# Four graph layers on one core: where TensorE transposes rows between rounds one and two, and when ScalarE copies them

## The reference, cut to what matters

```python
deg = segment_sum(ones, dst); dinv = rsqrt(deg); norm = dinv[src] * dinv[dst]
h = relu(segment_sum((x @ W1)[src] * norm[:, None], dst) + b1)
h = relu(segment_sum((h @ W2)[src] * norm[:, None], dst) + b2)
x = layernorm(x + h)
```

## Time and profile before

| | us |
|---|---|
| median of three runs | 4895.24 (4890.82 to 4900.14) |
| the profiled execution | 4889.19 |
| its span | 4887.5 |
| TensorE busy, matmuls | 3164.7 (65%) |
| GpSimd busy | 2620.9 (54%) |
| VectorE busy | 1604.3 (33%) |
| ScalarE busy | 1175.7 (24%) |
| mean granted TensorE clock | 0.748 of full speed |

### The profile page before, as it was taken

One profiled execution on the slowest core, in us unless ns is written; L12 is line 12 of the kernel. 1 busy time (PEld: TensorE's weight loads), 2 busy tenths in 40 slices (PEclk: granted clock), 3 DMA queues, 4 the chain that ended last, 5 costly groups with the idle time before them and its releaser, 6 DMA issues. The chain is left out here.

```text
span 4887.5 us, 63682 instructions
## 1 busy us (share of the span) xinstructions
PE 3164.7 (65%) x23462; PEld 2890.1 (59%) x23462; DVE 1604.3 (33%) x4664; ACT 1175.7 (24%) x1927; POOL 2620.9 (54%) x2640
## 2 busy tenths in 40 slices
PE   1599866885987788443333433355777777777777
PEld 1487755784886678443333323344766677767776
DVE  5588831232223222322212212244222222222224
ACT  4355420001000000122222222233222222222224
POOL 2555425555565555367666666624555555555550
PEclk8699977996998899666565566666777777777776
DMA  3344434664565456311111111112111111111111
GB/s 116 121 165 166 155 140 150 215 224 139 185 224 192 160 187 212 98 33 35 33 36 33 34 35 34 34 30 60 35 34 33 34 34 35 34 33 34 34 34 27
DMA packets 177090, 445.94 MB, mean 91 GB/s; under 512 B 68901, under 2 KB 115386, under 8 KB 156946
## 3 DMA queue, kind: packets, MB, share of 16 engines
q1 hardware_dynamic: 93332, 293.68, 16.6%
q0 software_dynamic: 83456, 148.23, 13.4%
HBM read 350.21 MB, written 91.50 MB: 90 GB/s over the span
## 5 line engine op out<-in xcount | busy, mean ns | idle before, releaser
L1216 PE MATMUL ps<-arena 128*125 128x288 bf16 x7448 | 1181.7, 303 | 171.9 <-issue 122.1
L736 POOL DMA_INDIRECT work_all<-parts_dram,idx_all x832 | 852.9, 1025 | 685.7 <-PE ps L1141 400.7
L1703 POOL DMA_INDIRECT arena<-table,idx_all x832 | 790.6, 950 | 779.7 <-DVE arena L1812 429.0
L1216 PEld LDWEIGHTS ps<-arena 128*125 128x125 bf16 x7448 | 1000.7, 146 | 247.8 <-issue 165.3
L1302 POOL DMA_INDIRECT arena<-table,idx_all x832 | 827.1, 994 | 409.5 <-issue 247.3
L1451 PE MATMUL ps<-arena 128*96 128x128 f32 x1664 | 339.5, 368 | 196.1 <-issue 139.4
L553 DVE TENSOR_TENSOR aggX<-aggX,ps 96x128 f32 x208 | 59.0, 284 | 1189.8 <-remote 730.3
L1451 PEld LDWEIGHTS ps<-arena 128*96 128x96 f32 x1664 | 296.6, 236 | 215.3 <-issue 191.2
L1873 PE MATMUL ps<-M,arena 96*128 96x96 f32 x1664 | 385.1, 329 | 21.5 <-issue 18.6
L1092 PE MATMUL ps<-arena,spare 128*128 128x245 bf16 x950 | 289.9, 312 | 86.6 <-issue 36.2
L1806 DVE COPY arena<-ps 128x1024 bf16<-128x1024 bf16 x104 | 71.9, 692 | 811.6 <-PE ps L1859 466.1
(11 more groups left out here) (341 smaller groups left out, 4860.1 us busy)
## 6 DMA issues: line engine op xcount, KB each, us to landing
arena<-blocks_dram SPq DMA_DIRECT2D x114, 1568.0 KB
blocks_dram<-arena SPq DMA_DIRECT2D x38, 1568.0 KB
arena<-table,idx_all POOLq DMA_INDIRECT x1664
parts_dram<-arena SPq DMA_DIRECT2D x28, 504.0 KB, 3.1
work_all<-parts_dram,idx_all POOLq DMA_INDIRECT x832
arena<-qtable SPq DMA_DIRECT2D x104, 72.0 KB
ea_dram<-arena SPq DMA_DIRECT2D x1, 4992.0 KB, 13.2
arena<-ea_dram SPq DMA_DIRECT2D x1, 4992.0 KB
```

The costliest lines, as they stand in the source:

```text
L736: eng.indirect_dma_start(out=gat_rows[kk % 3][:, u, :], out_offset=None, in_=parts_dram[:, :], in_offset=bass.IndirectOffsetOnAxis(ap=idx_ ...
L1216: last = nc.tensor.matmul(apply_ps[n % 2][0:w, :], blk[m % 3][:, b, 0:w], Hs[:, b, :], start=b == 0, stop=b == NB - 1)
L1703: eng.indirect_dma_start(out=rows[g % NROW][:, u, :], out_offset=None, in_=table[:, :], in_offset=bass.IndirectOffsetOnAxis(ap=idx_all[:, ...
```

## The change

TensorE: `turn` of chunk c-1 is issued behind the product of chunk c, at the end of round one; only that of the last chunk is left at the first block of round two. ScalarE: behind hi(c) and mid(c-1) it copies the transposed rows of chunk c-1, not of chunk c; the last copy is behind mid(6).

```diff
@@ block.scalar, round one
                         for c in range(NCH):
                             hi(r * NCH + c)
                             if c:
                                 mid(r * NCH + c - 1)
-                            turn(r * NCH + c)
+                                turn(r * NCH + c - 1)
                         mid(r * NCH + NCH - 1)
+                        turn(r * NCH + NCH - 1)
                         continue
@@ block.tensor, first block of a round
                                 if p == 0 and b % CB == 0:
                                     c = b // CB
-                                    if r == 2:
-                                        turn(NCH + c)
+                                    if r == 2 and c == 0:
+                                        turn(2 * NCH - 1)
                                     eng.wait_ge(parts_up, (r - 1) * NCH + c + 1)
@@ block.tensor, end of a round
                     eng.wait_ge(acc, n + 1)
                     for c in range(NEARLY if r > 1 else 0, NCH):
                         product(r, c)
+                        if r == 1 and c:
+                            turn(NCH + c - 1)
```

## The result

| | before | after |
|---|---|---|
| median of six runs, us | 4893.98 (4883.07 to 4900.14) | 4856.16 (4851.22 to 4861.00) |
| the profiled execution, us | 4889.19 | 4860.95 |
| its span, us | 4887.5 | 4859.2 |
| last `low` ends, behind the stage's first product | 63.29 | 25.54 |
| first gather of round two starts, behind it | 66.70 | 30.25 |

The ratio is 0.9924, with a 95% interval of 0.9910 to 0.9939. The medians are 37.8 us apart; 4857 was forecast.

A forecast was written before the change was run, and what follows sets the result against it. A ring of waits among TensorE, ScalarE and GpSimd between rounds one and two was the bound. 660.3 + 19.9 + 0.6 + 1.0 = 681.8, + 3.4 + 0.2 = 685.4 against 723.45; 4895.2 - 38 = 4857, upper end 4873, lower 2 us off 4850.

The forecast's parts named there:

- The ring: Between rounds one and two, TensorE, ScalarE and GpSimd wait on each other in turn, 8.04 us a turn.
- GpSimd's sum: Between rounds one and two: fourteen operations 19.9 us, hand-overs 0.6, one-hot 1.0; from 660.3, last low ends at 681.8 us.
- VectorE's one-hot: VectorE's `gathot`, moved to about 675.3 beside GpSimd's work, slows a rem there; 1.0 us taken once.
- TAB writes: VectorE's seven writes beside GpSimd's work between rounds one and two; nothing taken for them.
- The stores: Stores of parts before round two's first gather: 3.4 us plus 0.2 for the last one, gather at 685.4.
- the bound of 3.9 us on landing: A store of parts lands at most 3.9 us after its issue, over all 28; median 3.1.
- TensorE's hold: TensorE's transposes wait for ScalarE's copy three times, about 1.1 us each; products end about 6 us later, costing nothing.
- Rival A: TensorE falls to half clock in the interleaved stretch; last low near 694, gain 26 us, 4869; chance 0.10.
- The rule that transposes don't engage the full rate: For TensorE's interleaved stretch: transposes don't count as activity like matmuls, so it might run slow; no separate size.
- Rival B: GpSimd slowed between rounds one and two, or last stores queueing (3.9 us landing); gain 31 to 32 us, 4864; chance 0.12.
- Rival D: TensorE's instruction stock runs short during round two's gathers; 60 more starved matmuls cost 51 us, 4908; chance 0.03.
- The whole: Whole kernel: first gather of round two from 723.45 to 685.4, gain 38 us, median 4857.

The follow-up runs named there:

- kernel with two areas: The changed kernel with a second PSUM area for the odd chunks' transposes in round two; 4892.80 us, ratio 0.9908 to the kernel before.
- TensorE's extra work: The changed kernel with 49 more transposes on TensorE ahead of round two's first block; 3922.41 us, ratio 0.9906 to the kernel before.
- gaps in the gathers: The changed kernel with GpSimd's gather groups 1 and 2 waiting for TensorE each round; 3942.99 us, ratio 0.9957; on another chip 4831.17 us, 0.9894.

## Why the prediction was right

**The ring.** It was cut as said: GpSimd's pitch went from 8.04 to 3.03 us. The prediction gave both halves of the change a part in it. The runs show that TensorE's half suffices for the stage.

**GpSimd's sum.** Forecast: 21.5 us from first `rem` to last `low`; measured: 682.81 + 2.87 - 663.78 = 21.9. The 1.0 us taken for VectorE's one-hot was 2.44 - 1.46 = 0.98, at a `low` instead of a `rem`. The TAB writes cost nothing, as taken: every other GpSimd operation that stands by itself in the timeline took 1.46 or 1.47 us.

**The stores** were the mis-sized term: 0.2 us on top of 3.4 was taken, 1.3 measured. These 1.1 us are the larger part of what the stage lacks, 36.45 us instead of 38 (0.4 us more are in GpSimd's sum); the bound of 3.9 us on landing, from the 28 stores of before, was too low too (4.4 us at most after).

**TensorE's hold.** Three stops of about 1.1 us were forecast, before the transposes of chunks 1, 3 and 5. They are there, with 1.17, 0.99 and 0.99 us, and a fourth of 1.36 us stands before chunk 6. The trace names VectorE's TAB write for those of chunks 3 and 5, but the name goes by what ended last:

```profile
669.50 0.86 DVE L991 SCALAR_TENSOR_TENSOR TAB<-ps,dinv 128x672 f32<-128x672 f32 x1 [2.79 <-PE ps L1177]
...
671.71 0.90 ACT L808 ACTIVATE aggX<-ps 96x896 f32<-96x896 f32 x1
671.80 0.86 DVE L991 SCALAR_TENSOR_TENSOR TAB<-ps,dinv 128x672 f32<-128x672 f32 x1 [1.44 <-PE ps L1177]
...
672.75 0.94 PE L1134 MATMUL ps<-ident,TAB 128*96 128x128 f32 x7 [0.99 <-DVE TAB L991]
```

The write of chunk 3, which these transposes need, is that of 669.50; the one of 671.80 is chunk 4's, and they don't wait for it. ScalarE's copy of chunk 2 ends at 672.61, and the transposes start 0.14 us later. They start 0.14 us behind the end of a copy at the other three stops too. The kernel with two areas has none of the first three. The products queued behind the stops are those of chunks 3 and 5, not of 3 and 6 as the prediction has it; nothing stands behind the stop before chunk 5's transposes but chunk 6's. The last product ended at 17.4 us, forecast 17.3; the two-area run shows that the hold cost nothing.

**Rival A, the clock.** Out for the stretch that it spoke of: the granted clock was 1.00 for the first 18 us of the stage in all ten profiles that have both halves of the change and TensorE's stops. It stayed at 1.00 to the end in three of them (the change, the change once more, TensorE's extra work). In the other seven it went down between 18 and 22 us, where TensorE had stood idle 1.36 us before chunk 6's transposes. Here is the window 20 to 22 us behind the first product, with gaps in the gathers on the other chip (columns as in the earlier trace rows):

```profile
662.03:664.03 2.00, 1.31 (x7) 1.28 (x8) 0.00 (x0) 0.54 (x1) 1.86 (x2) 0.52 0.00 0
```

There chunk 6's transposes took 1.70 us instead of 0.94. It cost the stage nothing, since all products were done: the last `low` ended at 25.5 to 25.6 us with and without it, where GpSimd's order was the same. Since the same idle time stands in profiles without the fall, what decides it stays open. The rule that transposes don't engage the full rate (the Trainium skill, TensorE: Matmul & The Clock Gate, Part 4, PE-mode transpose) did not bite in the interleaved stretch; 49 transposes in a row, 5.4 us of nothing else, also kept the granted clock at 1.00, as the window of them in the run with TensorE's extra work shows:

```profile
593.80:599.20 5.40, 5.40 (x52) 5.40 (x50) 0.60 (x1) 2.12 (x3) 5.26 (x4) 1.00 0.40 124
```

**Rival B.** Its half on the stores took place in part (1.1 us more than forecast), its half on GpSimd did not.

**Rival D, the instruction supply.** The issue-bound stretch moved with the gathers, as the argument against it had it. Before, it ended at 779.06, 55.6 us behind the first gather (723.45); after, at 746.07, 55.7 us behind 690.39. So nothing was given back there. That the stretch is a want of instructions is the prediction's reading; the rows show only that TensorE waits for nothing else.

**The whole.** 38 forecast, 36.45 in the stage, 32.4 in round two of the two profiles, 37.8 between the medians. That the last is nearer to the forecast than the stage is luck within the spread of the runs.

## What to carry to other kernels

Where no engine is busy in a stage, follow one turn of the queues and ask for each neighbour in a queue whether the data asks for that order; here, moving work that had long been ready out from behind a late step gave 36 us, with the same instructions. Then cost the stage by the one engine that is left, its operations one after another, and count what starts at its end (here the first gather), not the engines' busy time. One half of a change may carry all of the gain, and only runs of the halves tell which. And where two things end within a tenth of a us, read in the kernel which one is waited for; the profile names the later.

## What the runs showed of the hardware

**In one of five sets of runs, on a chip of its own, the kernel before took 3960 us; it took 4881 to 4951 in the others.** The difference stands in TensorE's issue waits. The waits of TensorE over the whole span, longest first: the change, run once more, on a chip of the common kind, and then the kernel with TensorE's extra work on that chip (its only two such rows):

```profile
PE ps L1862 <- issue: 169.8, 218, 23.7
PE ps L1217 <- issue: 134.7, 174, 2.4
PE ps L1454 <- issue: 122.0, 111, 3.3
```

```profile
PE ps L1426 <- issue: 19.5, 1, 19.5
PE ps L1894 <- issue: 5.8, 1, 5.8
```

Summed over all lines, TensorE waits 702 to 839 us for issue in each profile on the other chips and 24 to 27 us in each of the four profiles on that chip. So the issue-bound stretch of rival D is no property of the kernel alone. The Trainium skill (Runtime: NRT & Kernel Launch, Instruction fetch mechanics) has the cost of going from one block of instructions to the next mostly hidden. If these waits are for instructions, the one chip agrees with it and the others don't. What is different about that chip no run here shows.

**VectorE and GpSimd.** A subtraction of VectorE with both inputs in SBUF took 0.86 us with GpSimd idle and 1.95 us when it started 0.2 us behind a `rem` of GpSimd, which kept its 1.46 us. The other way round, a `low` of GpSimd that started 0.1 us behind VectorE's one-hot took 2.44 us, and the one-hot 1.22 us, hardly more than in the earlier trace rows (1.16). In both cases the one that started second paid. VectorE's TAB write, with one input in PSUM, left GpSimd's 1.46 us as they were wherever they overlap.
